# Attention and feed-forward layer: output blocks between the key halves, both row maxima ahead of the even low part, layer norm work in odd steps

## The reference, cut to what matters

```
x = x + attn(layernorm(x))      # per batch element b of 8
    qkv = rms_norm(x) @ w_qkv                 # 256 -> 3 x 16 heads x 64
    sim = (q * 64 ** -0.5) @ k.T              # 512 x 512 per head
    out = softmax(sim) @ v ; out @ w_out
x = x + ffn(layernorm(x))
    gelu(x @ w1 + b1) @ w2 + b2, times the sum of the two renormalised top probabilities
```

## Time and profile before

| | |
|---|---|
| median of 3 runs | 1206.61 us (1205.59 to 1207.03) |
| the profiled execution's own time | 1207.99 us, its span 1206.2 us |
| TensorE busy (weight loads) | 1166.3 us, 97% (990.5 us, 82%) |
| VectorE busy | 1008.0 us, 84% |
| ScalarE busy | 872.4 us, 72% |
| GpSimd busy | 660.9 us, 55% |
| chain that ended last | PE 83%, DVE 7%, issue 2% |
| mean granted TensorE clock | 0.997 of full |

### The profile page before, as it was taken

One profiled execution on the slowest core, in us unless ns is written; L12 is line 12 of the kernel. 1 busy time (PEld: TensorE's weight loads), 2 busy tenths in 40 slices (PEclk: granted clock), 3 DMA queues, 4 the chain that ended last, 5 costly groups with the idle time before them and its releaser, 6 DMA issues.

```text
span 1206.2 us, 26861 instructions
## 1 busy us (share of the span) xinstructions
PE 1166.3 (97%) x10171; PEld 990.5 (82%) x10171; DVE 1008.0 (84%) x1738; ACT 872.4 (72%) x1897; POOL 660.9 (55%) x826
## 2 busy tenths in 40 slices
PE   9999999999999999999999999999999988999999
PEld 6778888888788888887888788878887876898898
DVE  7888888888988888888888988898889877777764
ACT  6888877888788778877888788878887866334432
POOL 5776565655565555655565556565655576222321
PEclk9999999999999999999999999999999989999999
DMA  4232112311231123112311222121212234424421
GB/s 133 78 90 74 36 36 71 86 30 36 62 88 36 37 71 89 36 37 71 89 37 36 71 70 56 36 65 51 71 35 63 54 88 139 131 90 135 129 73 36
DMA packets 58271, 82.95 MB, mean 69 GB/s; under 512 B 12576, under 2 KB 34592, under 8 KB 58144
## 3 DMA queue, kind: packets, MB, share of 16 engines
q1 hardware_dynamic: 58144, 81.24, 24.5%
HBM read 31.14 MB, written 16.25 MB: 39 GB/s over the span
## 4 chain that ended last, share of the span: by engine, by line
PE 83%; DVE 7%; issue 2%; POOL 1%; ACT 1%; DMA 1%; SPq 0%; ACTq 0%; POOLq 0%
PE ps L609 43%; PE ps L688 18%; PE ps L636 9%; PE ps L673 8%; PE ps L642 4%; DVE xres L1179 3%; DVE xn L1158 1%; DVE nat L1162 1%; PE ps L800 1%; ACT prob L941 0%; POOL prob L1036 0%; DMA xn<-blocks_scratch 0%; DVE ln_var L1145 0%; DVE ln_stats L1138 0%; POOL attT_lo L1073 0%
## 5 line engine op out<-in xcount | busy, mean ns | idle before, releaser
L1036 POOL TENSOR_SCALAR prob<-prob,rowinv 128x512 f32<-128x512 f32 x512 | 352.5, 701 | 382.8 <-DVE rowinv L1255 382.7
L941 ACT ACTIVATE prob<-ps,negmax 128x512 f32<-128x512 f32 x512 | 347.5, 686 | 51.1 <-DVE negmax L1250 40.1
L1162 DVE TENSOR_TENSOR pT_lo<-ps,pT_hi 128x512 fp32r<-128x512 f32 (+1 forms) x384 | 320.7, 863 | 65.6 <-ACT pT_hi L934 60.0
L1250 DVE TENSOR_REDUCE negmax<-ps 128x2 f32<-128x1024 f32 x256 | 310.8, 1214 | 1.3 <-PE ps L642 1.2
L931 ACT ACTIVATE pT_hi<-ps 128x1024 fp32r<-128x1024 f32 x128 | 131.7, 1029 | 129.1 <-issue 127.8
L673 PEld LDWEIGHTS ps<-identity,prob 64*128 64x128 f32 x4096 | 159.7, 139 | 64.1 <-issue 25.0
L636 PE MATMUL ps<-nat 64*128 64x512 f32 x1024 | 175.0, 413 | 16.8 <-DVE xres L1179 13.9
L673 PE MATMUL ps<-identity,prob 64*128 64x64 f32 x4096 | 178.4, 226 | 12.1 <-DVE nat L1162 9.6
L934 ACT ACTIVATE pT_hi<-ps 128x512 fp32r<-128x512 f32 x256 | 139.6, 605 | 5.5 <-PE ps L673 1.7
L688 PE MATMUL ps<-pT_hi,vbuf 128*128 128x512 f32 x512 | 138.5, 392 | 0.5 <-DVE pT_lo L1162 0.5
L688 PE MATMUL ps<-pT_lo,vbuf 128*128 128x512 f32 x512 | 137.0, 389 | 0.0
(11 more groups left out here) (115 smaller groups left out, 2286.9 us busy)
## 6 DMA issues: line engine op xcount, KB each, us to landing
att_hi_v<-halves_out SPq DMA_DIRECT2D x128, 128.0 KB, 2.3
att_lo_v<-halves_out SPq DMA_DIRECT2D x128, 128.0 KB, 2.3
blocks_scratch<-xblocks SPq DMA_DIRECT2D x15, 512.0 KB, 3.0
xn<-blocks_scratch SPq DMA_DIRECT2D x60, 128.0 KB, 2.8
xin<-in_x SPq DMA_DIRECT2D x32, 128.0 KB, 3.0
xres<-in_x SPq DMA_DIRECT2D x8, 512.0 KB, 3.5
x_scratch<-xres SPq DMA_DIRECT2D x8, 512.0 KB, 4.4
xin<-x_scratch SPq DMA_DIRECT2D x32, 128.0 KB, 3.1
```

Of the source, the lines that this page charges most:

```text
L941: act.activation(prob[:, n % NPROB, j * SEQ:(j + 1) * SEQ], ps[:, PS_SCORE[n % 2] + j, :], ACT.Exp, bias=negmax[:, n % 4, j:j + 1], accum_ ...
L1036: return pool.tensor_scalar(dst, src, scalar, 1.0, ALU.mult, ALU.mult)
L1162: return dve.tensor_tensor(dst, full, hi, ALU.subtract)
L1250: dve.tensor_reduce(negmax[:, n % 4, :], ps[:, PS_SCORE[n % 2]:PS_SCORE[n % 2] + 2, :], AX.X, ALU.max, negate=True).then_inc(s_max, 1)
```

## The change

It does three things. In even steps with a key block and an output block, TensorE now begins the key block (the three matmuls of the first half of the contraction, `begin_keys`), then makes the output block, then the last three matmuls of the key block; places 2 and 3 swap their meaning, and VectorE adds the output block to xres ahead of the query's low part. In even steps VectorE makes both row maxima ahead of the even tile's `transposed_lo`. The layer norm tasks stand in a table: statistics in slots 6, 7, 10, 11 (steps 3 and 5), normalising in slots 14 and 18 (steps 7 and 9), the router's weights in slot 15, turning in slots 22 and 23 (step 11). The power follows statistics task 3 by a step.

```
-NEXT_LN_SLOT = 5
+LN_SLOTS = {6: 0, 7: 1, 10: 2, 11: 3, 14: 6, 15: 10, 18: 8, 22: 9, 23: 13}
...
-            blocks += [(1, "q", step // 2 + 1), (2 if step else 4, "k", step // 2 + 1)]
+            blocks += [(1, "q", step // 2 + 1), (3 if step else 4, "k", step // 2 + 1)]
...
-                blocks += [(1, "out", quarter, 0), (2, "out", quarter, 1)]
+                blocks += [(1, "out", quarter, 0), (3, "out", quarter, 1)]
...
-                blocks.append((3, "out", quarter, since // 2))
+                blocks.append((2, "out", quarter, since // 2))
...
-            by_place = {1: odd_banks(step), 2: odd_banks(step) + 1, 3: PS_SCORE[0]}
+            by_place = {1: odd_banks(step), 2: PS_SCORE[0], 3: odd_banks(step) + 1}
...
-            b, step = divmod(slot - NEXT_LN_SLOT, SPB)
-            return (b + 1, step) if step < 14 and 0 <= b < B else None
+            b, rel = divmod(slot, SPB)
+            return (b + 1, LN_SLOTS[rel]) if rel in LN_SLOTS and 0 <= b < B else None
...
+            def begin_keys(step, block_no, place, kind, pair):
+
+                pe.wait_ge(s_ptlo, 2 * (2 * step - 3) + 2)
+                base = INNER + pair % PAIRS * P
+                if pair in (2, 4, 6):
+                    wait_weight_split(pe, pair - 2)
+                products(ps[:, aux_bank(block_no), :], [w[:, 0, base:base + P] for w in wqkv],
+                         [v[:, 0, :] for v in xT], True, False)
+
             def aux(step, block_no, place, kind, *args):
 
                 tile = 2 * step - 3
+                begun = kind == "k" and any(block[2] == "out" for block in aux_of(step)[0])
                 same_bank = [j for j in range(block_no) if aux_bank(j) == aux_bank(block_no)]
-                if place == 3:
+                if begun:
+                    pass
+                elif place == 2:
                     pe.wait_ge(s_exp, 2 * (2 * step) + 1)
...
-                        for k in range(KT):
+                        for k in range(1 if begun else 0, KT):
...
                 for block_of_aux in first:
+                    if block_of_aux[1:3] == (2, "out") and first[-1][2] == "k":
+                        begin_keys(step, *first[-1])
                     aux(step, *block_of_aux)
...
-                elif task and task[1] == 4:
+                elif task and task[0] and task[1] == 3:
                     powers(task[0] + 1)
...
                     if 0 <= 2 * step < NUNIT:
                         row_max(2 * step)
+                    if step % 2 == 0 and 0 <= 2 * step + 1 < NUNIT:
+                        row_max(2 * step + 1)
                     if 0 <= 2 * step - 2 < NUNIT:
                         transposed_lo(2 * step - 2)
-                    if 0 <= 2 * step + 1 < NUNIT:
+                    if step % 2 and 0 <= 2 * step + 1 < NUNIT:
                         row_max(2 * step + 1)
                     if 0 <= 2 * step < NUNIT:
                         row_inverse(2 * step)
-                for block_of_aux in early_blocks(step):
+                for block_of_aux in sorted(early_blocks(step), key=lambda block: block[1:3] != (2, "out")):
                     aux_done(*block_of_aux)
```

More of the change, by code:

```diff
@@ L429, in early_blocks @@
         def early_blocks(step):
-            return [block for block in aux_of(step)[0] if block[1:3] != (2, "k")]
+            return [block for block in aux_of(step)[0] if block[1:3] != (3, "k")]
         def pair_at(step):
@@ L453, in late_blocks @@
             return [block for block in aux_at.get(step, [])
-                    if block[1:3] == (2, "k") or block[1] > 3 and block[2] != "xt"]
+                    if block[1:3] == (3, "k") or block[1] > 3 and block[2] != "xt"]
         def odd_tiles(n):
@@ L626, in scores @@
                     for block in aux_of(n // 2 - 1)[0]:
-                        if block[1:3] == (3, "out"):
+                        if block[1:3] == (2, "out"):
                             pe.wait_ge(s_added, added_no(*block[3:]))
@@ L707, in first_product @@
                 return ins
+            def begin_keys(step, block_no, place, kind, pair):
[5 more added lines that the diff above has]
+                         [v[:, 0, :] for v in xT], True, False)
             def aux(step, block_no, place, kind, *args):
                 tile = 2 * step - 3
+                begun = kind == "k" and any(block[2] == "out" for block in aux_of(step)[0])
                 same_bank = [j for j in range(block_no) if aux_bank(j) == aux_bank(block_no)]
-                if place == 3:
+                if begun:
+                    pass
+                elif place == 2:
                     pe.wait_ge(s_exp, 2 * (2 * step) + 1)
-                elif place <= 2 and 0 <= tile < NUNIT:
-                    pe.wait_ge(s_ptlo, 2 * tile + place)
+                elif place in (1, 3) and 0 <= tile < NUNIT:
+                    pe.wait_ge(s_ptlo, 2 * tile + (1 if place == 1 else 2))
                 elif same_bank:
```

## The result

| | before | after |
|---|---|---|
| median | 1206.24 us of 4 runs (1205.59 to 1207.03) | 1171.66 us of 4 runs (1170.61 to 1172.36) |
| ratio, with its 95% interval | | 0.9712 (0.9695 to 0.9729) |
| profiled execution, its span | 1207.99, 1206.2 us | 1172.36, 1170.6 us |

A forecast was written before the change was run, and what follows sets the result against it. TensorE, 97% busy, bounds the kernel, so only closing holes in its stream saves time. -25.4 + 3.5 - 1.4 - 12.0 = -35.3 us takes the profiled 1208.0 to 1172.7, median forecast 1171.3 us, range 1167.5 to 1184.

The forecast's parts named there:

- Part 1: Output block between the key halves: scores no longer wait for VectorE's add into xres, 59 x 0.43 = 25.4 us gained.
- the new wait: Output block's weight load waits for the exponent's first half: 0.06 us a pair, 3.5 us back, at most 10.0.
- the sum: All gains and costs of the change together: -25.4 + 3.5 - 1.4 - 12.0 = -35.3 us.
- Part 2: Both maxima ahead of the even low part: 1.4 us from three pairs without output block, only slack in the others.
- Part 3: Layer norm in odd steps: two long pairs shortened, 12.0 us, no cost under VectorE's 2.17 us idle per pair.
- rival B: Layer norm stall moves with the work, pieces near 2 us push the even maximum: 1183.3 us, chance 0.07.
- The port rule: VectorE and GpSimd lock a shared port: at worst normalisations take 2.22 us in odd steps, sum within 1 us.
- Queues: SyncE's queue at step 12: regroupings behind the blocks' store land by 6.0 us, needed at 7.7; hidden.
- A: TensorE waits for the first exponent half ahead of the output block, say 0.3 us: 1185.5 us, chance 0.09.
- C: VectorE's add comes no earlier and the xres wait stays: 1193.2 us, chance 0.04.
- D: Slower: output block in effect waits for the exponent's second half, 0.79 us in each of 59 pairs: 1214.4 us, chance 0.03.
- the last sign of being wrong: TensorE's granted clock below full within the attention part would show the forecast wrong.

The follow-up runs named there:

- the kernel without it: Four key matmuls ahead of the output block and two behind, against the changed kernel: 1169.01 us, 0.9682 of before.
- the undoing of part 2: Second row maximum behind the even tile's low part again in even steps, against the changed kernel: 1175.75 us, 0.9745 of before.

## Why the prediction was right, point by point

- **What bounds the kernel.** Right: both kinds of holes closed, and TensorE is now busy for all of a pair.
- **Part 1, the gain of 0.43 us a pair.** Right, 0.95 to 0.52 us for the transposes. The add was to come at 6.38 us and came at 6.45, and the margin was to be 0.25 us and is 0.27; undone, the whole wait came back.
- **Part 1, the new wait, 0.06 us.** Right in the cost, 0.05 us by the first output matmul and 0.06 by the kernel without it, and in the mechanism: the load starts at 490.02, 0.05 us before the matmul, as the prediction had it. But 0.06 was a choice between the bounds 0 and 0.17, not worked out from a row, so that it came out to 0.01 us is luck in part. Wrong in how it would look: the text said that the wait's length would be the 0.06. The waits in the list are 0.21 us each, because the weight load is idle that long; the matmul behind it lost only 0.05. 59 x (0.43 - 0.05) = 22.4 us against the 21.9 of the sum.
- **Part 2.** Low: the three pairs without output block were to give 1.4 us and that stretch gave 1.63, 0.43 in the first and 0.60 us in each of the other two (14.93 to 14.33). The sum took the 0.48 us that ScalarE waited for what TensorE would win; with the second maximum behind again all of it is gone, but no run shows why it is 0.60. The step that failed is "in pairs with an output block this only adds slack". It is true of the kernel before, where the odd step started later. In the shorter pair 0.05 us of it are load-bearing, 3 us, as the undoing of part 2 shows. It isn't missing from the sum only because the new order was in place.
- **Part 2, the even low part, 0.7 us of slack.** Right, with more to spare: it ends at 491.42, the transposes start at 492.35, 0.93 us later.
- **Part 3, 12.0 us and no cost.** Right, 11.8 us. The layer norm pieces never asked for the cover of 2.17 us in full: behind the normalisation at 543.92, below, the next reciprocal starts at once, so that piece is as large as the first idle time (1.15 us in the plain pair) allows, and the second idle time is hardly touched. The piece priced highest, "at most 2.04" for the statistics in step 5, adds 13.27 - 12.42 = 0.85 us to its pair. The 1.62 us it was taken from are those of a pair that also held the normalisation of 1.12 us at 546.92. So rival B had less for it than the prediction gave it.

```profile
543.26 0.73 DVE L1176 TENSOR_TENSOR vbuf<-ps,vbuf 128x256 fp32r<-128x256 f32 x2
543.92 1.11 DVE L1172 TENSOR_SCALAR xn<-xin,ln_mv,ln_scale 128x256 f32<-128x256 f32 x2
545.14 0.17 DVE L1269 RECIPROCAL rowinv<-rowsum 128x2 f32<-128x2 f32 x1
```

- **The port rule.** Its worst case didn't occur: the two normalisations took 1.11 us with GpSimd's scaling beside them (a pair of scalings of 1.44 us from 543.44), as in the earlier trace rows. With layer norm back in its old slots 2.09 us came back next to GpSimd's two-input add (543.66), and 1.11 stayed next to its scaling (535.27). Taken one by one the rows say more, before and after:

```profile
555.34 1.52 DVE L1158 TENSOR_SCALAR xn<-xin,ln_mv,ln_scale 128x256 f32<-128x256 f32 x1
```

```profile
544.24 0.79 DVE L1172 TENSOR_SCALAR xn<-xin,ln_mv,ln_scale 128x256 f32<-128x256 f32 x1
544.11 0.76 POOL L1050 TENSOR_SCALAR prob<-prob,rowinv 128x512 f32<-128x512 f32 x1
```

One normalisation takes 0.40 us at the shortest. The first row, beside the add of 555.42 to 556.71, ends at 556.86, 0.15 us behind the add; the second ends at 545.03, 0.16 behind the scaling. So the normalisation is held up by either instruction until that one has ended, and what differs is how long that one is, 1.29 or some 0.7 us: the 1.11 us of the odd step already have one such hold in them. By the Trainium skill, "SBUF — State Buffer", section "Who interferes with whom", the lock of the shared port pair is taken on VectorE's side by operations in a two-port mode or with two SBUF inputs; these have one, so by that page it would be the mode, which no row shows. That the hold lasts as long as GpSimd's instruction agrees with the exclusive lock that the prediction cites.
- **Queues.** The step that failed is "Weight and residual loads are issued elsewhere". In the first batch element a weight load is issued at slot 20, right behind the store. The count of issues lacked it, the landing was taken as 3.0 us, and it was up to 6.4. Predicted 6.0 us against a need at 7.7; it was 9.7. The cost is 1.1 us once. In the other elements the issues were as counted, but behind the store alone the landing took up to 4.5 us and not 3.0: 7.2 us against a need at 7.6, so 0.4 us and not 1.7 hid it.
- **The drain and the rest.** The sum gave them nothing; they gave 0.94 and 0.36 us, which makes up for that 1.1 us. Of the 0.94 us, 0.91 stand in the last pair and go with the granted clock of the two executions (last section), not with the change. The forecast for the profiled execution was 1172.7 us and it took 1172.36; this closeness is in part luck, errors of about 1 us that cancel.

**Rivals.** A wait for the exponent of 0.3 us (A), the layer norm stall moving along (B), and the xres wait staying (C) are ruled out by pairs of 14.89 us throughout. The slower one (D) is ruled out by them too. It named the right place, and its price of 0.66 us a pair for the break-even was right, but not the mechanism: even with no key matmul ahead, the output block starts 0.14 us behind the first half of the exponent, and never waits for the second. The granted clock was 1.00 through the repeating part (67.25 to 947.38), so the last sign of being wrong didn't show either.

## What to carry to other kernels

A block that must wait for another engine can be put into the middle of another, and how far in decides: with the rest of the change in place, three matmuls ahead gave 2.9% over before, none lost 0.4%, and the trace of before had told where the first half of the exponent ends. When work is moved to a later slot, list what every queue holds at that slot for each batch element, the first and last among them: the one pair that got longer had a load that no other element has. Slack read in the old timeline is that of the old period: once a pair is 0.4 us shorter, an edit that "only adds slack" may carry some of the gain.

## What the runs showed of the hardware

**The drain and the granted clock.** In the drain TensorE is idle for 1 to 2 us at a time, and behind that the granted clock falls. The repeating part and the drain of the changed kernel, by windows:

```profile
67.25:947.38 880.13, 879.17 (x8261) 725.78 (x8261) 783.84 (x1247) 738.93 (x1655) 537.96 (x675) 1.00 0.23 61
947.38:979.50 32.12, 27.57 (x228) 22.34 (x229) 23.55 (x43) 20.15 (x38) 22.94 (x27) 0.95 0.34 95
```

Behind the 1.86 us of idle time the output matmuls start 0.12 us apart from 953.97 on, and then 0.21 us apart from 955.09 on:

```profile
954.81 0.28 PE L609 MATMUL ps<-wout_lo,attT_hi 128*128 128x256 f32 x1
...
955.09 0.42 PE L609 MATMUL ps<-wout_hi,attT_lo 128*128 128x256 f32 x1
```

So for a part of this stretch the lower of the two levels (1.2 GHz, not 2.4) was granted. How much of it was low differs between executions, and the length of the last pair goes with it. That pair before, in the changed kernel, and with the weight load moved:

```profile
981.68:999.33 17.65, 14.08 (x116) 11.19 (x116) 12.12 (x17) 10.97 (x25) 13.57 (x16) 0.81 0.23 60
947.38:964.12 16.74, 13.20 (x117) 10.27 (x118) 12.04 (x17) 10.61 (x24) 13.57 (x16) 0.90 0.24 64
946.16:963.93 17.77, 14.20 (x116) 11.24 (x117) 12.03 (x17) 10.61 (x24) 13.60 (x16) 0.81 0.24 60
```

A mean clock of 0.81 goes with 17.65 and 17.77 us, and with 17.94 with the query's low part ahead of the add; 0.90 goes with 16.74 us, with 16.75 in the changed kernel's repeat and 16.90 with the store behind the regrouping. TensorE is busy 0.88 us longer before than after, for the same matmuls. So the drain's 0.94 us goes with the clock that this execution was granted and isn't a gain of the change, and so does the microsecond by which kernels with the same end of attention differ. What decides between the two lengths of low clock stays open, and so does which of them the executions without a profile had.
